# Perceiver layer on one core: token rows scattered three times per shared pair, last x rows and first token tiles moved ahead, one low part between mask operations

## The reference

```python
x = x + xattn(layernorm(x), ctx)       # softmax over ctx, batch softmax of the row maxima, 2048x512 projection
x = x + attn(layernorm(x))             # 16 heads of 32, causal over 64 tokens, Wq Wk Wv Wm
h = layernorm(x)
probs = softmax(h @ w_router.T)        # 8 experts, top 2, weights normalised
moe   = sum over the 2 experts of weight * (square(relu(h @ w1[e].T)) @ w2[e].T)
shared = square(relu(h @ ws1.T)) @ ws2.T          # 512 -> 1024 -> 512
x = x + shared + moe
```

## Time and profile before

| | us |
|---|---|
| three runs | 1353.44, 1356.63, 1359.42 |
| median | 1356.63 |
| the profiled execution, its own time | 1352.82 |
| its span, first to last instruction | 1351.1 |
| PE busy | 1315.8 (97%) |
| DVE busy | 715.5 (53%) |
| ACT busy | 341.4 (25%) |
| POOL busy | 160.8 (12%) |

### The profile page before, as it was taken

One profiled execution on the slowest core, in us unless ns is written; L12 is line 12 of the kernel. 1 busy time (PEld: TensorE's weight loads), 2 busy tenths in 40 slices (PEclk: granted clock), 3 DMA queues, 4 the chain that ended last, 5 costly groups with the idle time before them and its releaser, 6 DMA issues.

```text
span 1351.1 us, 20762 instructions
## 1 busy us (share of the span) xinstructions
PE 1315.8 (97%) x7203; PEld 811.7 (60%) x7204; DVE 715.5 (53%) x1339; ACT 341.4 (25%) x604; POOL 160.8 (12%) x169
## 2 busy tenths in 40 slices
PE   5889999999999999999999999999999999999999
PEld 2334444444443444456888888899897666666643
DVE  3335545644444444467977778757443444444436
ACT  2101111211111111133444443442122222222210
POOL 0000000000000000013000005502430000000045
PEclk9999999999999999999999999999999999999999
DMA  9999999999999999831366753131659999999797
GB/s 366 385 394 395 395 391 389 393 392 387 386 385 381 375 364 371 332 141 71 141 242 242 269 207 137 63 132 72 260 207 320 295 308 314 295 303 302 226 327 255
DMA packets 123041, 392.18 MB, mean 290 GB/s; under 512 B 12240, under 2 KB 34768, under 8 KB 122864
## 3 DMA queue, kind: packets, MB, share of 16 engines
q1 hardware_dynamic: 117872, 374.79, 76.0%
q0 software_dynamic: 5120, 16.78, 3.4%
HBM read 333.32 MB, written 58.20 MB: 290 GB/s over the span
## 4 chain that ended last, share of the span: by engine, by line
PE 88%; SPq 6%; DMA 3%; DVE 2%; issue 1%; ACT 0%; POOL 0%; POOLq 0%; DVEq 0%; ACTq 0%
PE ps L1844 12%; PE ps L1908 11%; PE ps L1784 11%; PE ps L1898 10%; PE ps L2187 7%; PE ps L1794 4%; PE ps L1805 4%; PE ps L1745 4%; PE ps L1797 4%; PE ps L2193 3%; PE ps L2190 3%; PE ps L2196 3%; PE ps L2262 2%; PE ps L2254 2%; SPq L409 2%; PE ps L1944 2%
## 5 line engine op out<-in xcount | busy, mean ns | idle before, releaser
L749 ACT ACTIVATE arena<-ps 128x512 f32<-128x512 f32 (+1 forms) x135 | 70.5, 535 | 588.8 <-PE ps L1745 263.3
L1844 PE MATMUL ps<-arena 128*64 128x512 f32 (+1 forms) x832 | 194.0, 599 | 2.0 <-DMA arena<-ctx_n 1.8
L1784 PE MATMUL ps<-arena 128*64 128x512 f32 (+1 forms) x1024 | 179.4, 505 | 11.0 <-DMA arena<-ctx_t 8.1
L1908 PE MATMUL ps<-split 128*128 128x256 f32 x1344 | 170.6, 285 | 1.2 <-DVE split L1259 1.1
L1908 PEld LDWEIGHTS ps<-split 128*128 128x128 f32 x1344 | 163.7, 191 | 7.2 <-issue 6.3
L1898 PE MATMUL ps<-split 128*128 128x512 f32 x648 | 157.5, 396 | 0.3 <-DVE arena L1326 0.3
L1784 PEld LDWEIGHTS ps<-arena 128*64 128x64 f32 x1024 | 65.9, 138 | 133.0 <-issue 121.0
L1185 DVE SCALAR_TENSOR_TENSOR arena<-arena,hbar 128x512 f32<-128x512 f32 x128 | 90.5, 748 | 95.2 <-PE ps L1805 90.6
L1898 PEld LDWEIGHTS ps<-split 128*128 128x128 f32 x648 | 119.0, 188 | 28.3 <-issue 3.5
L1844 PEld LDWEIGHTS ps<-arena 128*64 128x64 f32 (+1 forms) x832 | 58.5, 138 | 116.5 <-issue 111.9
L1118 DVE TENSOR_REDUCE small<-ps 128x1 f32<-128x1601 f32 x16 | 29.2, 1825 | 148.8 <-PE ps L1784 148.8
(11 more groups left out here) (195 smaller groups left out, 1660.5 us busy)
## 6 DMA issues: line engine op xcount, KB each, us to landing
arena<-ctx_t SPq DMA_DIRECT2D x128, 800.5 KB, 18.8
arena<-ctx_n SPq DMA_DIRECT2D x128, 768.0 KB, 15.6
split<-parts_low SPq DMA_DIRECT2D x39, 768.0 KB, 7.0
split<-parts_low SPq DMA_DIRECT2D x39, 512.0 KB, 4.5
moe_in<-zero SPq DMA_DIRECT2D x3, 3328.0 KB, 13.6
moe_out<-arena SPq DMA_DIRECT2D x39, 256.0 KB, 4.3
stage_raw<-w1t SPq DMA_DIRECT2D x8, 768.0 KB, 5.5
parts_high<-split SPq DMA_DIRECT2D x8, 768.0 KB, 7.0
```

The source lines that it names most:

```text
L1784: last = mm(bank(n)[S * h:S * (h + 1), 0:w], qT[:, k, S * h:S * (h + 1)], ctxT[h][:, k, at_j:at_j + w], start=(k == 0), stop=(k == KD - 1))
L1844: last = mm(bank(7)[S * h:S * (h + 1), :], ET[0:w, c, S * h:S * (h + 1)], ctxN[h][0:w, c, :], start=(c == 0), stop=(c == JC - 1))
L1908: last = mm(dst[:, 2 * P * m:2 * P * (m + 1)], w[a][:, k, c], tokens[b][:, k, :], start=(k + i == 0), stop=(k == KD - 1 and i == 2))
```

## The change

Three things.

Stage B: in `start_b` on DVE the low part of h1 of tile 2 stands between the mask and the maxima, and that of tile 3 between the maxima and the subtraction. ACT's `h1_high` for half 0 waits for one V projection fewer.

Scatter: in pair p = 1 the calls stay as they are. In p = 2 and p = 3 there are three: ahead of the residual adds, between the residual adds and the low parts, and behind the low parts. Pair p = 4 has none. So token pairs 2 to 4 go in p = 2, and 5 to 7 in p = 3. In the last pair DVE transposes the first token tile before the residual add of tile 8.

SP: the store of x rows 12 to 15 stands ahead of the load of w1 of expert 4; the first token tile is loaded before rows 4 to 7 are stored and w2 of expert 7 is loaded; then the second token tile, and only then w1 of expert 0.

```diff
@@ SP
-            for i in range(2):
-                r = slice(TH // 2 * i, TH // 2 * (i + 1))
-                sp.wait_ge(x3_ready, TH // 2 * (i + 1))
-                sp.dma_start(away[:, r, :], X[:, r, :]).then_inc(x3_out[i], 16)
-                sp.wait_ge(x3_out[i], 16)
-                load_w2(ARENA + i * KD * D, 6 + i, 7 + i)
-                if i == 0:
-                    sp.wait_ge(h2lo_ready, 6)
-                    load_w1(2, 3)
-                    sp.wait_ge(routed, EXPERTS)
-                    load_w2(3 * KD * D, 3, 4)
-                    sp.wait_ge(h2lo_ready, 10)
-                    load_w1(3, 4)
-                    sp.wait_ge(h2lo_ready, TA)
-                    load_w1(4, 5)
+            sp.wait_ge(x3_ready, TH // 2)
+            store_rows(slice(0, TH // 2))
+            sp.wait_ge(x3_out, 16)
+            load_w2(ARENA, 6, 7)
+            sp.wait_ge(h2lo_ready, 6)
+            load_w1(2, 3)
+            sp.wait_ge(routed, EXPERTS)
+            load_w2(3 * KD * D, 3, 4)
+            sp.wait_ge(h2lo_ready, 10)
+            load_w1(3, 4)
             sp.wait_ge(hs_ready, T)
-            sp.dma_start(away[:, TR:T, :], X[:, TR:T, :]).then_inc(x3_out[0], 16)
+            store_rows(slice(TR, T))
+            sp.wait_ge(h2lo_ready, TA)
+            load_w1(4, 5)
...
             e = expert_of(0)
-            sp.wait_ge(sh_done, 4 * (TA // 2))
-            load_w1(0, 1)
-            sp.wait_ge(x3_out[0], 32)
+            sp.wait_ge(x3_out, 32)
             load_low(e, 0)
...
             load_slots(0)
+            sp.wait_ge(x3_ready, TH)
+            store_rows(slice(TH // 2, TH))
+            sp.wait_ge(x3_out, 48)
+            load_w2(ARENA + KD * D, 7, 8)
+            sp.wait_ge(xgT_ready, 1)
+            load_slots(1)
+            sp.wait_ge(sh_done, 4 * (TA // 2))
+            load_w1(0, 1)
             load_w2(0 * KD * D, 0, 2)
             load_w2(2 * KD * D, 2, 3)
             e = expert_of(1)
-            sp.wait_ge(xgT_ready, 1)
-            load_slots(1)
             load_w2(4 * KD * D, 4, 6)
@@ ACT
-                    act.wait_ge(v_done, 2 * n)
+                    act.wait_ge(v_done, 2 * n - 1 + i)
@@ DVE, start_b
-                masked_scores(0, True)
+                mask(0, True)
                 h1_low(2, 0)
+                row_maxima(0)
                 h1_low(3, 1)
+                less_maximum(0)
@@ DVE, shared network
-            def shared(p, scatter):
+            def shared(p, scatter=None):
                 shared_start(p)
+                if scatter is None:
+                    shared_residuals(p)
+                    shared_rest(p)
+                    return
                 scattered_norm(scatter)
+                shared_residuals(p)
+                scattered_norm(scatter + 1)
                 shared_rest(p)
-                scattered_norm(scatter + 1)
+                scattered_norm(scatter + 2)
...
             with dve.Fori(2, 4) as p:
-                shared(p, scatter=2 * p - 2)
-            shared(4, scatter=6)
+                shared(p, scatter=3 * p - 4)
+            shared(4)
             last_pair = TA // 2 - 1
             square(last_pair, 0)
             square(last_pair, 1)
-            residual_c(TA - 4, 0)
             dve.wait_ge(slots_zeroed, 48)
             tokens_T(0)
+            residual_c(TA - 4, 0)
             tokens_low(0)
```

More of the change, by code:

```diff
@@ L370, in perceiver_layer @@
         shared_done, x3_ready = sem("shared_done"), sem("x3_ready")
-        x3_out, x3_back = [sem(f"x3_out{i}") for i in range(2)], sem("x3_back")
+        x3_out, x3_back = sem("x3_out"), sem("x3_back")
         xg_in = sem("xg_in")
@@ L531, in _, with store_rows @@
             away = x_away.rearrange("(t p) d -> p t d", p=P)
-            for i in range(2):
-                r = slice(TH // 2 * i, TH // 2 * (i + 1))
-                sp.wait_ge(x3_ready, TH // 2 * (i + 1))
-                sp.dma_start(away[:, r, :], X[:, r, :]).then_inc(x3_out[i], 16)
-                sp.wait_ge(x3_out[i], 16)
-                load_w2(ARENA + i * KD * D, 6 + i, 7 + i)
-                if i == 0:
-                    sp.wait_ge(h2lo_ready, 6)
-                    load_w1(2, 3)
-                    sp.wait_ge(routed, EXPERTS)
-                    load_w2(3 * KD * D, 3, 4)
-                    sp.wait_ge(h2lo_ready, 10)
-                    load_w1(3, 4)
-                    sp.wait_ge(h2lo_ready, TA)
-                    load_w1(4, 5)
+            def store_rows(r):
+                sp.dma_start(away[:, r, :], X[:, r, :]).then_inc(x3_out, 16)
+            sp.wait_ge(x3_ready, TH // 2)
[8 more added lines that the diff above has]
+            load_w1(3, 4)
             sp.wait_ge(hs_ready, T)
-            sp.dma_start(away[:, TR:T, :], X[:, TR:T, :]).then_inc(x3_out[0], 16)
+            store_rows(slice(TR, T))
+            sp.wait_ge(h2lo_ready, TA)
+            load_w1(4, 5)
             def expert_of(g):
@@ L1329, in masked_scores, with mask @@
             def masked_scores(t, first):
+                mask(t, first)
+                row_maxima(t)
+                less_maximum(t)
+            def mask(t, first):
                 dve.wait_ge(s_done, t + 1)
@@ L1335, in masked_scores, with row_maxima, less_maximum @@
                                        ).then_inc(smask_ready, 1)
+            def row_maxima(t):
                 dve.wait_ge(smask_ready, t + 1)
                 v.tensor_reduce(rmax[:, :], sm, AX, ALU.max).then_inc(smax_ready, 1)
+            def less_maximum(t):
                 dve.wait_ge(smax_ready, t + 1)
@@ L1542, in shared_start, with shared_residuals, shared_rest @@
                     h2_low(p + 1, i)
-            def shared_rest(p):
+            def shared_residuals(p):
                 residual_c(2 * p - 2, 0)
                 residual_c(2 * p - 1, 1)
+            def shared_rest(p):
                 shared_low(p, 0)
@@ L1645, in _ @@
             scattered_norm(0)
+            shared_residuals(1)
             shared_rest(1)
```

## The result

The changed kernel takes 1360.15 us (median of 21 runs), the kernel before, run beside it, 1355.65 (21 runs): ratio 1.0040, interval 1.0023 to 1.0056. That is inside the 0.5% of the prediction, all but the upper end of the interval, but the sign is the other one: -3.6 us was forecast, and about +5 measured (medians 4.5 apart, 5.4 by the ratio). The profiled execution took 1374.58 us (span 1372.9), 14 more than the median.

What follows compares the result with a forecast made beforehand. PE was taken to bound the kernel, busy 1315.8 of 1351.1 us. Terms +0.8 + 0.5 - 4.0 - 0.9 = -3.6 us gave 1349.2 profiled, 1353.0 as a median; range 1348.5 to 1360.

Steps and rivals of the forecast that it cites:

- A: Attention's opening in stage B: Q projection's wait goes, but a later square root delays the K projection; +0.8 us, bounds -1.1 to +1.4.
- I count no fall: Opening: PE's 1.9 us wait before the K projection brings no clock fall, which would add 1.8 us.
- B: Three scatters per shared pair in p = 2 and 3: the middle landing barely stalls PE; +0.5 us, bounds 0 to +5.5.
- The slower rival: Shared pair p = 3: middle scatter lands late (6.0 us), B 5.5, sum +1.4, 1358.0 us; chance 0.15.
- C: First expert token tile: earlier last scatter lets it start straight after the shared matmuls at full clock; -4.0 us, bounds -4.0 to 0.
- In time by 2.7: First token tile: the last w1 load, issued at 1011.8, lands at 1020, before PE ends its shared work at 1022.67.
- D: Third and fourth expert tiles: earlier w2 loads clear the queue for tile 3's slots; -0.9 us, bounds -1.26 to 0.
- The third rival: First token tile still late: last w1 load or low parts hold PE, C and D gone; +1.3, 1357.9 us; chance 0.12.

Runs made afterwards that it cites:

- e2: Changed kernel with two scatters per shared pair again, the last one between the residual adds of p = 4; 4.7 us slower than the kernel before.
- f5: Changed kernel with the middle scatter of p = 2 and 3 moved behind the low parts, new opening kept; 4.2 us slower than the kernel before.
- f7: Kernel before with only the changed opening of stage B (DVE's order and ACT's earlier rounding); ratio 1.0008 to the kernel before.
- g4: Changed kernel with w2 of experts 6 and 3 and w1 of experts 2 and 3 loaded behind the store of rows 12 to 15; ratio 0.9996.
- e4: Changed kernel with the loads of w1 of expert 2 and w2 of expert 3 moved behind the store of rows 12 to 15; B +4.61 us.
- e3: Changed kernel with two scatters per shared pair, the last two early in p = 4, and the old opening; 3.6 us slower than the kernel before.
- f8: Kernel before with only the changed opening, and ACT's rounding of the first weight set moved behind the square root; ratio 1.0001.
- g2: g1 with tile 3's slot load ahead of SP's wait for tile 0's up projection and its low weights; time as g1's (1356.49 and 1356.19 us).
- g1: e3 with SP's w1 load of expert 0 moved to right behind the first tile's slot load; ratio 1.0019 to the kernel before.

## Why the prediction was wrong, step by step

**A, +0.8 forecast, +1.94 measured.** The chain was right link by link: Q's wait goes, ACT's square root is 0.73 late against the V projection (forecast 0.8), K waits 1.93 (1.9) and leaves 0.74 late (0.8). The subtraction took 1.55 us, the 635.85 to 637.4 of the forecast. Missed is "I count no fall": in five of the six profiles with a K wait of 1.91 to 1.99 us (changed kernel, e2, f5, f7, g4) the clock fell and 24 matmuls took 4.28 to 4.63 us; in e4 it did not. It costs 1.2 us (A is 1.94 to 2.01 with it, 0.70 in e4) and stood among my bounds.

**B, +0.5 forecast, +7.17 measured: the step that failed.** The prediction let "token pair 4" take "the place in the DMA backlog that pair 3 had, so DVE's wait for its odd tile ends near 975.2". It ended at 981.94, 5.4 us late even when the 1.35 by which PE is later in all (979.02 against 977.67) is taken off. The landing behind it was then quick, near what I had chosen: POOL's issue ended at 985.65 and DVE went on at 987.68, 2.03 us later (1.8 forecast for a quiet queue). So I had bounded the wrong term: the one landing, and not the start of the row of landings. Three scatters in a period of 22.4 us share two buffers; each late landing delays the next issue, and token pair 3's second tile lands at 971.34, 7.1 us after its issue (963.20 + 1.05), beside the loads that SP had sent. And "the weight loads that made the queue busy have drained by then" was wrong by one load: w1 of expert 3 was issued at 974.58, 0.1 us after the start of POOL's second issue for the very tile (974.48) that landed at 981.94. Before, this load went out at 969.18. It is DVE's own wait that moved it: SP waits for the low part of h (`h2lo_ready`), which now stands behind the landing of 971.34. g4 shows the part of the loads by taking them away (B 0), e2 and e3 that of the third scatter (B 0), f5 that the place within the pair is not it. The slower rival, at 0.15, had the place and a stall of 3.7 us (it was 4.93), but hung it on the middle landing too.

The Trainium skill (DMA: Bandwidth & Descriptors, SWDGE vs HWDGE vs iDMA) says that each DMA engine goes round between its software and hardware queues. The runs do not bear out what I drew from it, that a scatter is then free of the loads: 6 to 7 us beside them, about 2 without.

B alone is not the whole miss, though: with B at 0 and the rest of the change kept, e2 is still at 1.0035. The forecast had C as a gain of its own, and it is not one.

**C, -4.0 forecast, -3.98 measured; but not for the reason I gave, so by luck.** "In time by 2.7" was worked out for a w1 load issued at 1011.8. In the changed kernel it goes out at 1020.32, when PE, 8.5 us later than before (1020.12 against 1011.60), frees its place. Where no stall gives SP that time, its queue decides: e3 sends the same load at 1019.67, g4 at 1019.96, though PE is ready near 1010 to 1013, and C is +2.7 and -1.3. I had put one wait ahead of it (the transpose) and listed "rows 4 to 7 are stored at 1001 as before" at nothing; but their store now stands behind the first slot load, so behind the last scatter's landing, and w2 of expert 7 behind the store's own landing.

**C and D are one account.** In the table, C + D is -4.54, -3.35, -3.15, -2.80 and -4.34 in the five kernels with a stall B of 4.6 to 7.4 us, and -0.3 to +5.4 in the eight without. My reading, which no single run shows: the first tiles need a fixed amount of weights, slots and stores in SP's serial order, and PE idle that goes in one place comes back in the next unless PE itself is late. What is clear of noise is e3: A and B at 0, SP's order and the early tile kept, and a ratio of 1.0027 (1.0015 to 1.0038). In the kernel before the DMA share is 0.96 to 1.06 in every 6 us from 1024 to 1054, and f7 and f8, which change nothing there, had C -2.5 and -2.2 and D +2.2 and +3.0. Part of that is the clock: the first tile's idle was 2.17 us before, with half clock behind it, and 1.27 (f7) and 1.56 (f8) with none; f7's rest of +1.70 and g4's of +2.52 go with half clock behind idles of 1.30 and 2.70 us before the fourth tile. So no variant without a stall ahead won the 4 us that I priced at the earlier trace rows. The third rival (first tile still late) had this cause, and I gave it 0.12.

**D, -0.9 forecast, -0.56 measured,** with +0.42 behind it. The sign fits, and the share of the DMA engines in 1042 to 1056 fell from 0.97 to 0.81. But the w2 loads went out from 1021.17, not "from 1012", against a PE that was 4 us later, not 4 earlier, so the number is luck. The slots of tile 3 still land some 4.4 us after their last issue. Whether a fuller queue or SP's order makes them late stays open; g2 points to the order.

**The numbers.** PE's matmuls of p = 3 start at 977.67 in the earlier trace rows, where I wrote 977.8; nothing hangs on it. Forecast -3.6, measured +4.99: B is off by 6.7, A by 1.1, D and the rest by 0.8. The median of 1360.15 is just above my range, drawn at the slower rival plus 2. B's upper end of 5.5 was no end (stall and clock, 3.7 + 1.8, came as 4.93 + 2.24), and A's clock fall was not added to it.

What stays open: what decides on a clock fall behind an idle of 1.3 to 2.5 us (e4's K wait of 1.94 had none); the last 22.7 us of the changed kernel's profiled execution; and whether an order of SP's queue exists in which C stays a gain without the stall. One with the store of rows 4 to 7 and w2 of expert 7 ahead of the wait for the last scatter was not tried.

## What to carry to other kernels

When an edit puts one more round trip of a DMA into a loop, follow the buffers over several iterations and count round trips per period, rather than price one landing; list every load of the other queues with its issue time beside each. An idle gap of the bounding engine at the head of a stretch in which the DMA engines are near full is not a gain of its length: ask which load is next late, and read the issuing queue's waits for landings as well as its order. And a gain that appears in the changed kernel may live on another part's loss; only undoing the loss shows it (here e2 and e3).

## What the runs showed of the hardware that I had not expected

- An indirect scatter of one tile (two DMAs) landed 2.0 us after its second issue on a quiet queue (changed kernel, 985.65 to 987.68; g4, 964.69 to 966.73) and 6.5 to 7.1 us after it beside weight loads (changed kernel, 975.44 to 981.94 and 964.25 to 971.34). One load of w1, 1 MB, issued 0.1 us after the start of the second issue was enough (e4, 971.26 to 977.27).
- A PE idle of 1.91 to 1.99 us at the K projection was followed by half clock five times in six. The length alone does not settle it. In the 14 profiles, from 628 to 652 and from 950 to 1070, the seven idles of 0.94 to 1.15 us were not followed by half clock, and the eleven of 2.70 to 8.17 us all were; between them it went both ways: 1.30 (f7, fourth tile) and 2.17 us (before, first tile) were, 2.02 (f5) and 2.09 (e2, both fourth tile) and 2.45 us (g4, first tile) were not.
- A 1 MB store took 8.5 us (g1, 1012.66 to 1021.12) and, behind 5 MB of weight loads, 13.7 us (g4, 1003.48 to 1017.16) from issue to the next load that waited for it; before it took 4.3 (1001.00 to 1005.29).
